# Edge counting by sub-tile parts of the destinations, and stage ends without the GpSimd drain, in a graph and mixture-of-experts network on one core

## The reference, cut to what matters

```python
x, src, dst          # x: 3125 nodes of 256 features; 100000 edges src -> dst, sorted by dst
x = x + L0_gnn(layernorm(x), node_type, src, dst)   # embedding of the node type, two GAT layers with 4 heads
x = x + L0_ffn(layernorm(x))                        # 8 experts, one per node, with a capacity
x = x + L1_gnn(layernorm(x), src, dst)              # gated graph layer: two segment sums over dst
x = x + L1_ffn(layernorm(x))                        # shared hidden layer, one of 8 output experts per node
```

## Time and profile before

| | us |
|---|---|
| median of 3 runs | 3466.37 |
| lowest and highest run | 3463.25, 3470.77 |
| the profiled execution's own time | 3458.42 |
| its span, first to last instruction | 3456.7 |

### The profile page before, as it was taken

How to read it: one execution, slowest core, us unless ns; L and a number is a source line. 1 busy time by engine, 2 the same in 40 slices (tenths; PEclk the granted TensorE clock), 3 DMA queues, 4 the chain that set the end, 5 groups by cost and what they waited for, 6 DMA issues and landing times. The chain is left out here.

```text
span 3456.7 us, 52465 instructions
## 1 busy us (share of the span) xinstructions
PE 2747.0 (79%) x18168; PEld 1414.3 (41%) x18169; DVE 2561.1 (74%) x5315; ACT 1164.8 (34%) x2305; POOL 1386.3 (40%) x1623
## 2 busy tenths in 40 slices
PE   6999969999969999944886856777777777774698
PEld 3555533433443433442564411333333333333586
DVE  7999979999959999973843957677776766762354
ACT  6777740000020000021111124555555555552232
POOL 2555530000000000002046877777777777731343
PEclk9999989999979999957998966666666666766899
DMA  6000010000040000004232577888888888843411
GB/s 203 9 9 9 9 32 13 13 13 13 5 71 13 13 13 14 5 12 132 80 93 61 160 232 235 241 241 240 242 241 240 240 240 242 241 138 126 153 48 32
DMA packets 243127, 377.64 MB, mean 109 GB/s; under 512 B 83648, under 2 KB 172917, under 8 KB 241067
## 3 DMA queue, kind: packets, MB, share of 16 engines
q0 software_dynamic: 79440, 247.13, 24.1%
q1 hardware_dynamic: 148795, 112.25, 11.2%
q10 hardware_dynamic: 14624, 14.88, 1.3%
HBM read 324.13 MB, written 51.75 MB: 109 GB/s over the span
## 5 line engine op out<-in xcount | busy, mean ns | idle before, releaser
L1111 PE MATMUL dense_p_o<-dense_W,feat 128*32 128x512 f32 (+1 forms) x8400 | 879.8, 543 | 23.8 <-DVE dense_W L1053 23.7
L1053 DVE SCALAR_TENSOR_TENSOR dense_W<-layer_B,steep,cnt 128x512 f32<-128x512 f32 (+1 forms) x1400 | 848.7, 678 | 51.2 <-PE dense_p_o L1111 47.8
L2246 POOL DMA_INDIRECT strips_G<-tab_d,ixq x784 | 756.0, 964 | 243.2 <-issue 237.4
L1111 PEld LDWEIGHTS dense_p_o<-dense_W,feat 128*32 128x32 f32 x8400 | 361.6, 109 | 512.9 <-DVE dense_W L1053 226.0
L2415 PE MATMUL strips_p_sg<-strips_sv,strips_oh 128*32 128x512 f32 x2000 | 384.8, 854 | 107.4 <-DVE strips_sv L2286 107.4
L1495 POOL MEMSET route_up<- 128x128 f32 x1 | 0.2, 206 | 1006.9 <-POOLq L145 1006.9
L2403 PE MATMUL strips_p_b<-strips_wrs,strips_ohT 96*128 96x256 bf16 x1000 | 210.0, 350 | 233.6 <-DVE strips_ohT L2257 208.9
L2276 DVE TENSOR_TENSOR strips_tv<-strips_G,strips_p_b 128x1024 f32<-128x1024 f32 (+1 forms) x250 | 264.2, 1057 | 176.1 <-PE strips_p_b L2403 73.3
L2286 DVE TENSOR_TENSOR strips_sv<-strips_G,strips_p_s 128x1024 f32<-128x1024 f32 (+1 forms) x250 | 262.9, 1052 | 142.8 <-ACT strips_p_s L2360 142.3
L2360 ACT ACTIVATE strips_p_s<-strips_tv 128x1024 f32<-128x1024 f32 (+1 forms) x250 | 225.0, 900 | 301.9 <-DVE strips_sv L2286 287.8
L693 POOL TENSOR_SCALAR mix_L<-mix_back,encode_lowT 128x128 bf16<-128x128 f32 x392 | 249.9, 655 | 170.5 <-PE mix_p_c L851 170.4
(11 more groups left out here) (422 smaller groups left out, 3784.6 us busy)
## 6 DMA issues: line engine op xcount, KB each, us to landing
strips_row<-dlr_d SPq DMA_DIRECT2D x250, 96.0 KB
experts_ew<-in_ew SPq DMA_DIRECT2D x16, 1024.0 KB
strips_G<-tab_d,ixq POOLq DMA_INDIRECT x784
layer_B<-rise_d SPq DMA_DIRECT2D x12, 1024.0 KB
dense_Wd<-in_fWd ACTq DMA_DIRECT2D x1, 8192.0 KB
tab_d<-feat SPq DMA_DIRECT2D x50, 128.0 KB, 2.5
tab_d<-gated_in_rowg SPq DMA_DIRECT2D x25, 256.0 KB, 2.0
wr_d<-gated_in_wp SPq DMA_DIRECT2D x25, 192.0 KB
```

The costliest lines, as they stand in the source:

```text
L1053: o = nc.vector.scalar_tensor_tensor(out=out, in0=rise, scalar=C.steep[:, q * H + h:q * H + h + 1], in1=count, op0=ALU.max, op1=ALU.mult)
L1111: m = nc.tensor.matmul(p_o[c % 2][h * MT:(h + 1) * MT, a, 0:n], feat[:, q, h, lo:lo + MT], W[t % 2][:, h, 0:n], start=(q == 0), stop=(q == ...
L2246: gp.indirect_dma_start(out=G[n % RING][:, part(g) + j, :], out_offset=None, in_=C.tab3[:, :], in_offset=bass.IndirectOffsetOnAxis(ap=inde ...
```

## The change

It has three parts.

1. **Sub-tile spans.** Since the edges are sorted, sub-tile j of a group holds only some of the window's destinations. The table `SPAN` gives each sub-tile its part: 0 to 8, 2 to 12, 6 to 16 and 8 to 20. The key becomes `rel * NB + hi`, so that a span of destinations is a run of columns: 200, 250, 250 and 300 instead of 500. `one_hots` compares only the span. The last sub-tile (`FULL`) goes first and is multiplied over all 500 columns, since it starts the accumulation; the 200 columns below its span are set to zero once for each of the four buffers, before the loop. The other three are multiplied over their spans. `add` now reads the counts from PSUM with a step of 25 words between neighbouring elements, 20 at a time. `bad` now also tests that each sub-tile lies in its span.
2. **Block ends.** All 15 `nc.Block()` become `nc.Block(no_gpsimd_drain=True)`: GpSimd does not drain there; the other engines drain, and the barrier behind it is of semaphore instructions alone.
3. **Clearing.** The barrier behind the clearing of semaphores becomes `all_engine_barrier(sem_only=True)`. The drain of GpSimd ahead of the clearing, which belongs to `clear_and_free_semaphores`, stays.

```diff
+SPAN = [(0, 8), (2, 12), (6, 16), (8, 20)]
+FULL = ET - 1
+SPAN_AT = [NB * sum(hi - lo for lo, hi in SPAN[:j]) for j in range(ET)]
+RW = SPAN_AT[FULL] + CK
...
             nc.clear_and_free_semaphores(sems)
-            nc.all_engine_barrier()
+            nc.all_engine_barrier(sem_only=True)
...
-        with nc.Block() as block:
+        with nc.Block(no_gpsimd_drain=True) as block:
...
+                    for j, (lo, hi_) in enumerate(SPAN):
+                        nc.vector.memset(lower[:, j:j + 1], float(lo)).then_inc(s_lim, 1)
+                        nc.vector.memset(upper[:, j:j + 1], float(hi_)).then_inc(s_lim, 1)
...
-                    nc.vector.scalar_tensor_tensor(out=key[:, :, :], in0=hi[:, :, :], scalar=float(CW), in1=rel[:, :, :], op0=ALU.mult, op1=ALU.add).then_inc(s_key, 1)
+                    nc.vector.scalar_tensor_tensor(out=key[:, :, :], in0=rel[:, :, :], scalar=float(NB), in1=hi[:, :, :], op0=ALU.mult, op1=ALU.add).then_inc(s_key, 1)
...
-        R = [sb(f"R{k}", [P, ET, CK], BF16) for k in range(NL)]
+        R = [sb(f"R{k}", [P, RW], BF16) for k in range(NL)]
...
+        order = [FULL] + list(range(FULL))
+
+        def own(g, j):
+            lo, hi = SPAN[j]
+            at = SPAN_AT[j] + (lo * NB if j == FULL else 0)
+            return R[g % NL][:, at:at + (hi - lo) * NB]
+
+        def near_keys(j):
+            return ramp16[:, SPAN[j][0] * NB:SPAN[j][1] * NB]
+
+        def whole(g, j):
+            return R[g % NL][:, SPAN_AT[j]:RW] if j == FULL else own(g, j)
+
+        def to_count(g, j):
+            lo, hi = (0, CW) if j == FULL else SPAN[j]
+            return p_c[g % 2][:, lo * NB:hi * NB]
+
+        def counted(g):
+            return p_c[g % 2][:, 0:CK].rearrange("p (d b) -> p b d", b=NB)
...
-                    for j in range(ET):
-                        nc.vector.tensor_scalar(R[g % NL][:, j, :], ramp16[:, :], keyT[:, i, j * CP + p:j * CP + p + 1], None, ALU.is_equal).then_inc(s_oh, 1)
+                    for j in order:
+                        nc.vector.tensor_scalar(own(g, j), near_keys(j), keyT[:, i, j * CP + p:j * CP + p + 1], None, ALU.is_equal).then_inc(s_oh, 1)
...
-                    nc.vector.tensor_tensor(a, a, p_c[g % 2][:, 0:CK].rearrange("p (b d) -> p b d", d=CW), ALU.add).then_inc(s_add, 1)
+                    nc.vector.tensor_tensor(a, a, counted(g), ALU.add).then_inc(s_add, 1)
...
                 nc.vector.memset(one[:, :], 1.0).then_inc(s_one, 1)
+                for k in range(NL):
+                    nc.vector.memset(R[k][:, SPAN_AT[FULL]:RW], 0.0).then_inc(s_clear, 1)
+                v.wait_ge(s_clear, NL)
...
-                    for j in range(ET):
-                        t = nc.tensor.matmul(p_c[g % 2][:, 0:CK], L[g % NL][:, j, :], R[g % NL][:, j, :], start=(j == 0), stop=(j == ET - 1))
+                    for j in order:
+                        t = nc.tensor.matmul(to_count(g, j), L[g % NL][:, j, :], whole(g, j), start=(j == FULL), stop=(j == order[-1]))
```

More of the change, by code:

```diff
@@ L419, in stage_encode_count @@
             hi = sb("hi", [CP, 2, EG], I32); d0 = sb("d0", [CP, 2]); rel = sb("rel", [CP, 2, EG]); low = sb("low", [CP, 2, EG]); key = sb("key", [CP, 2, EG])
[L420 removed]
+            same = hi[:, :, 0:EG - RUN + 1].bitcast(F32); reach = sb("reach", [CP, 2, ET]); begins = sb("begins", [CP, 2, ET]); upper = sb("upper", [CP, ET]); lower = sb("lower", [CP, ET]); runs = sb("runs", [CP, 2]); bad = sb("bad", [CP, 1])
             ranked = sb("ranked", [P, 1])
```

40 lines of the change are left out of this document (23 added, 17 removed).

## The result

| | before | changed |
|---|---|---|
| median, us (4 runs each) | 3467.43 | 3413.30 |
| lowest and highest run, us | 3463.25, 3470.77 | 3411.76, 3419.45 |
| the profiled execution's own time, us | 3458.42 | 3411.76 |
| its span, us | 3456.7 | 3410.1 |

The ratio is 0.9848, with a 95% interval from 0.9831 to 0.9865. The change saves 54 us between the medians and 46.6 us between the profiled spans. I had forecast 3432 us, a saving of 34 us, in a range from 3403 to 3478. 3413 us lies in that range, but outside the forecast's own 3424 to 3444, and closer to the 3408 of rival 1. The sign was right, and so was the mechanism of the mix stage, whose loop gained a little less than I said. The mechanism of the block ends was wrong: where I had written a loss, they gained.

What follows compares the result with a forecast made beforehand. VectorE (96% busy, TensorE 93%) set the mix stage's pace, with the hand-off loop deciding. Terms -46 + 1.2 + 0.5 + 10.7 - 0.7 = -34 gave 3424 us profiled, 3432 us median with 8 us added; range 3403 to 3478.

Steps and rivals of the forecast that it cites:

- rival 1: Block ends: the drain's work vanishes and the clearing's drain does not do it; 13.1 us saved, 3408 us, chance 0.15.
- Loop of the mix stage: Mix stage, one `second` to the next: 17.18 us falls to 15.13, 1.9 of 2.05 taken over 24 periods, -46 us.
- a late hand-off: Mix stage loop: 1.9 of the 2.05 us saved per block is taken, since some hand-off will be late.
- the size of the one-hots: Mix stage, VectorE: 1000 columns compared instead of 2000 saves 0.51 us per group, 4.1 per block; work falls to 12.3.
- my own list of signs: Mix stage: period near 15.3 us, one-hots 0.13 apart, add 0.66; wrong if VectorE over 90% busy or period above 16.
- my term of 1.02 us: Mix stage loop: add 5 and `inverse` behind it until `scaled` starts on ScalarE, 1.02 us, kept unchanged.
- The add: Mix stage, VectorE: reading PSUM in steps of 25 words costs nothing, within nothing to 0.53 us per add.
- Rivals 2 and 3: Mix stage's add: strided read costs about half (3445 us, chance 0.16) or all (3480 us, chance 0.22) of the SBUF row.
- The counts: Mix stage, TensorE: a count goes from 0.85 to 0.52 us, work per block from 15.9 to 13.3.
- The start of the stage and the preparation: Four memsets ahead of `mix_off` and the wait behind them, +1.2 us; three more small steps for `bad`, +0.5 us.
- The block ends: GpSimd's drain work moves to the clearing's drain: 0 where GpSimd came last, gated_in +2.1, strips +8.6, together +10.7 us.
- The barriers' 0.7 us: Barriers at 20 clearings lose a GpSimd drain and block ends gain a semaphore instruction: -0.7 us, between -2 and +1.

Runs made afterwards that it cites:

- e6: Changed kernel with narrow one-hots but all four matmuls of a count 500 columns wide: 3765.56 us, ratio 0.9932 to the kernel before.
- e5: Kernel before with only the new key order and the add's strided PSUM read, 500 columns everywhere: 3792.26 us beside 3793.41, ratio 0.9996.
- e2: Kernel before with only the new block ends and clearing barrier, counting as before: 3773.62 us, ratio 0.9956 to the kernel before.
- e9: Changed kernel with a plain drain ending GpSimd's program in six stages: 3749.95 us, single run; changed kernel 3735.34 on another chip.
- e10: Changed kernel with a plain GpSimd drain behind each block's barrier, ahead of the clearing's: 3763.19 us, single run, 27.9 over the changed kernel on another chip.
- e3: Changed kernel with the barrier behind each clearing draining all engines again: 3742.88 us, ratio 0.9874 to the kernel before.
- e1: Changed kernel with the old block ends and clearing barrier, so the spans alone: 3746.78 us beside 3794.69, ratio 0.9878 to the kernel before.
- e12: Changed kernel, GpSimd taking group 2 of eight and some own one-hots, root adding 1e-5 as bias, `features` behind add 7: 3385.88 us, ratio 0.9759 to before.
- e7: Changed kernel with matmuls of the spans but all four one-hots 500 columns wide: 3762.43 us, ratio 0.9919 to the kernel before.

## Why the prediction was right, and where it was wrong

**Loop of the mix stage.** The terms, forecast and read from the changed kernel's timeline:

| step | forecast, us | measured, us |
|---|---|---|
| `second` | 3.55 | 3.56 |
| count 5 until add 5 | 0.81 | 0.81 |
| add 5 until `scaled` | 1.02 | 1.31 |
| `scaled` to the end of the last copy | 4.26 | 4.25 |
| until `first` | 0.06 | 0.05 |
| `first` to `second` | 5.43 | 5.52 |
| sum | 15.13 | 15.50 |

That ScalarE's copy takes VectorE's place as what `first` waits for was right, and so were four of the six terms. I allowed 0.15 us for a late hand-off and it was 0.37, within my bounds (the lower of which, a quarter of 49 us lost, is -37 and not -36): 24 x 0.2 = 5 us of the forecast 46 are missing. With the memsets the stage saved 40.75 us against a forecast of 44.8.

**The step that failed in the loop is the size of the one-hots**, "0.26 us for 500 columns", taken as 0.52 ns a column. That was one width, divided. In the records of single instructions the next one-hot starts 181, 197, 206 and 260 ns (medians) behind one of 200, 250, 300 and 500 columns: some 130 ns fixed and 0.26 ns a column. Halving the columns takes a fifth to a quarter off, not half. Four take 0.8 us instead of 0.52, and VectorE's work in a block is 0.9 x 15.5 = 14.0 us instead of 12.3. By that my own list of signs speaks against the forecast in two places: the one-hots were to start 0.13 us apart, and it was to be wrong if VectorE stayed busy for over 90%, which it is with 72.44 of 80 us (90.6%). The loop decided even so: its block is 15.50 us, 1.5 us above VectorE's work. Most of it is hidden, but one group stands between add 3 and add 4, ahead of `moments`. In the timeline add 3 starts at 213.10, when count 3 is there; add 4 at 214.63; `moments` at 215.21; the root, which waited 2.60 us for them, at 216.96; and behind the `near` of that step `scaled` at 219.00. The way over add 5 and `inverse`, the only one that my term of 1.02 us had in it, would have allowed some 218.7. So `scaled` came 0.3 us late by the 0.3 us that one group of one-hots takes more than I said: the wait that ends last is that for the moments, over the root and `near`. In e6, where the one-hots are as narrow but the counts long, it is `inverse` again that `scaled` waits for, 22 times between 100 and 450 us; the changed kernel has no such wait:

```profile
ACT mix_z L828 <- DVE mix_off L766: 5.3, 22, 0.2
```

That fits its block: 15.13 + 4 x 0.33 = 16.45 us, beside 16.51 measured. That one group of one-hots makes the moments late is argued from these two traces; no run took the group away by itself.

**The add.** I took nothing for the strided read and called it the weakest choice. It was right, as e5 shows with nothing else changed: 665 ns in both, ratio 0.9996. Rivals 2 and 3 fall with it. The choice had luck in it: my reason, that PSUM has room for single words, was not tested. The Trainium skill's figure of 1.73 ns per column ("Vector Engine (DVE) Microarchitecture Reference", section 5.2) is measured in SBUF; e5 shows that it does not hold for this read of PSUM. "SBUF — State Buffer" of the Trainium skill (section "Door 1: The DMA port swizzle") says that PSUM has lines of 8 bytes and that non-contiguous access to it slows down matmuls. No run here has such a matmul, and VectorE's read shows no such cost.

**The counts** took 0.68 us from the first start to the last end instead of 1.01, the 0.33 less that I forecast.

**The start of the stage and the preparation.** The memsets and the step behind them, in the changed kernel:

```profile
52.96 1.07 DVE L776 MEMSET mix_R<- 128x250 uint32 x4
54.07 0.19 DVE L779 SCALAR_TENSOR_TENSOR mix_off<-encode_mv,encode_rstd 128x25 f32<-128x25 f32 x1
```

From 52.96 to 54.07 is 1.1 us, against 1.2. The preparation took 2.6 us longer. From the copy of `wg` to the subtraction of `key` it is 1.58 us instead of 1.34, so the three new steps explain 0.24, half of what I said. The rest is no work of the change: the copy itself, which waits for TensorE's product of the weights, starts at 29.76 instead of 26.85, and with the old steps the preparation took 49.64 us before, 50.93 in e2 and 55.35 in e5, and with the new ones 50.18 to 53.43.

**The block ends: this part of the forecast was wrong.** The step is "with the first one gone the work falls to it": I read that the clearing's drain was short only because another stood right ahead of it. A plain drain does work that way: it takes 2110, 4142 and 4782 ns in route, experts and tiles at the end of the program (e9), and 2109 and 4142 in the first two behind the barrier (e10). But the clearing's drain is not one of them, and takes 138 ns at most (after, e3). Rival 1 was right, to which I gave 0.15. It named 13.1 us saved in four stages; route, experts, pick and tiles saved 15.0, and gated_in 1.0, which is not the drain's (e9 has the drain and 121.76 us). The barriers' 0.7 us are within these. Where I had written +10.0 for the ends, these five stages read -16.0. Two readings behind the step were loose. 3211.69 in pick is the end of the last DMA's issue, not of the DMA; that the drain is no wait for data follows from the kernel, where GpSimd waits for all 25 scatters (L2891) before its program ends. And 84 ns for each indirect DMA fits 25 to 58 of them, but not strips, with 834 and a drain of 7.1 us (e10). Nor do the 2546 ns of gated_in with its 25, which are 2092 behind the barrier. A plain drain waits for GpSimd's running work too, which may be the difference there. The mix stage has no indirect DMA, and yet a drain of 3.2 us before: GpSimd's last one-hots of `low` end at 475.60, and the drain, begun at 472.7, ends 0.3 us behind them:

```profile
470.61 4.99 POOL L693 TENSOR_SCALAR mix_L<-mix_back,encode_lowT 128x128 bf16<-128x128 f32 x8 [2.77 <-PE mix_p_c L851]
```
```profile
L672 POOLq DRAIN  x1: 3175/3175/3175, 472.7 to 472.7; - x1
```

**The whole.** The profiled span lost 46.6 us and the terms had said 34.3. The difference of -12.3 is made of -26.0 for the ends, +4.0 for the mix stage with its memsets, +2.1 for the preparation, and +7.5 in `between` and strips, in which nothing but the ends changed. Those last are scatter of single executions: `between` took 44.19 us before, but 48.0 in e5 and 49.0 in e1, which have the old ends too, and 46.9 to 49.2 in the others; strips took 1149 us in the changed kernel and 1143 in e12 with the same code there, both on chips of the faster kind. So errors of opposite sign stood in the sum: a gain of the loop taken 4 us too large, and the ends taken for a loss. The second is by far the larger; with the scatter set against it, the profiled execution came 12.3 us below the forecast for it. The median is 18.7 us below, because I had also added 8 us for its distance from the profiled execution, and that distance was 1.5 us this time. That 3413 lies in the stated range is owed in part to luck: the range was wide enough for rival 1, which was what the ends did.

## What to carry to other kernels

Before taking a price per column from one instruction, find a second width: the fixed part decides what a narrower tile is worth, and here it was some two thirds of the narrow one. When two engines are both near full, cutting work on one gives only what the other allows; cut both, then trace the loop of hand-offs from one start of an operation to its next, since an engine busy for 95% of a stage need not be what bounds it. In that loop moving work behind the instruction that someone waits for was worth 9.5 us, and taking more work off the same engine elsewhere was worth nothing.

## What the runs showed of the hardware

- A plain drain of GpSimd takes 82 to 84 ns for each indirect DMA of the stage, with 25 to 58 of them, whether it stands at the end of GpSimd's program (2110 ns in route, e9) or behind a barrier (2109 ns, e10). This does not go on: behind the 834 of strips it took 7077 ns (e10). It also waits for work that GpSimd still has running (3175 ns at the end of the mix stage before, where there is no indirect DMA). The drain that belongs to the clearing of semaphores doesn't do it (138 ns at most), and once it and the clearing have run a plain drain finds nothing left (34 to 51 ns, e3). Whether the clearing's drain or the clear itself ends the account was not tried.
- VectorE's add reads PSUM in steps of 25 words as fast as contiguously: 665 ns for 500 elements either way (e5).
- VectorE's 16-bit one-hots cost some 130 ns and 0.26 ns a column from start to start, between 200 and 500 columns (the changed kernel and e7).
- The strips stage took 1143 to 1149 us in three traces (before, changed, e12) and 1466 to 1481 in the eleven others, on three other chips; the mix stage of the changed kernel took the same on both kinds (397.49 and 397.99 us). What differs there is open.
